# w_repr and b_repr as one replicated array, per-channel patch weights over three banks, and the bias from TensorE, in the opening of a one-layer vision tower

## The chip, the cores and the metric

The kernel runs on one core of one Trainium2 chip. The metric is the device time of one execution in microseconds, and the median of several runs counts. Before the change the median of three runs is 330.68 us, from 330.09 to 334.6 us. The engines are PE (TensorE; PEld is its weight load), DVE (VectorE), ACT (ScalarE), POOL (GpSimd) and SP (SyncE, which here only issues DMAs). A name with q (ACTq, SPq) is the sequencer of that engine.

## The reference, cut to what matters

The input is 32 images of 3 x 96 x 96, cut into 16 x 16 patches: 36 tokens an image, 1152 in all. The change touches only the first step, the tokens.

```
y = jnp.einsum('bchw,rc->bhwr', x, W_repr) + b_repr
y = y.reshape(bs, h, ph, w, pw, R)
y = y.transpose(5, 0, 1, 3, 2, 4).reshape(R, bs, h * w, ph * pw)
out = jnp.einsum('rbnp,rep->bne', y, W_proj) + b_proj.sum(axis=0)
...
h = h + attn(_layernorm(h), W_qkv, W_out)       # 12 heads of 64, over each image's 36 tokens
h = h + ffn(_layernorm(h), gate_w, gate_b, w1, b1, w2, b2)   # 8 experts of 768, one per token
```

R is 5 and the embedding is 192 wide. The first product is linear in x, so the kernel folds it: for each channel c an effective patch weight weff[c] = sum over r of W_repr[r, c] * W_proj[r], and a constant row, the bias, which is the sum over r and over the 256 pixels of b_repr[r] * W_proj[r], plus the sum of b_proj.

## The kernel before, in words

The tokens go in four blocks (NB) of 288, each in three tiles (NT) of 96. Ahead of the blocks stands an opening, which does for block 0 what block b does for block b+1: tokens, layer norm, transposition, the first query and key heads, and the values. The blocks are a hardware loop on each engine, and after them comes the expert layer over gathered tiles of 128 tokens. The order of work is written by hand, engine by engine, with semaphores between them. Each engine works through its program in order, so an instruction that waits holds up all that stands behind it on that engine.

**The opening, by engine.** SP issues the loads in order: W_repr and b_repr spread over all 128 partitions (wr, br), the patch weights (wp, 960 KB), the patches of block 0 (xb, 864 KB), b_proj, the query/key/value weights in two column pieces of two DMAs each (wq, pieces 0 and 1), W_out and the gate. wp shares its bytes with a later tile, so the trace calls it late, as it does weff. DVE makes weff for channels 0 and 1, going through r and alternating between the two channels (L936, L938). ACT makes the five scaled pieces of channel 2 (L691) and POOL adds them up (L1179). DVE then makes wb, the pixels' share of the bias (L945, L947). PE adds it over the partitions with a tile of ones (L536 to L538), and DVE copies it out of PSUM (L954). PE makes the tokens of a tile in six products (L413), which DVE takes with the bias added (L859), followed by the layer-norm statistics (L848, L850). POOL makes 1/std from them (L1196, L1199), DVE the normalised rows (L854), and PE transposes them (L421, L422). ACT rounds the transposed rows to the single-pass format (L705, L707) and DVE takes the rest (L867, L868). Only then can the heads start (L428), which are sums of five single-pass products: for them the weights too are split in a rounded part (ACT, L695, L696) and a rest (DVE, split_wq, L875 and L877).

**What runs beside it.** After its casts of wq piece 1 ACT issues the load of the first expert weights w1, two DMAs of 3072 KB (L699, L700). w1A_in shares its bytes with the scaled pieces of channel 2, so ACT also waits for weff. SP issues the patches of block 1 (L374) when all three tiles of normalised rows are there. POOL copies the tokens (keep_h, L1234) and then issues three indirect DMAs (L1211), which write single words of the expert lists to HBM. Here the ones of the opening write to spare places.

**Where w1 is needed.** In each of the first three blocks ACT rounds a third of w1 in between its attention work: round_w1 part 0 in step 1 (L715), part 1 in step 3 (L718), part 2 in step 5 (L720). Part 0 waits on one semaphore for both DMAs of w1. Behind it on ACT stand the copies of the query and key heads out of PSUM (L724, L729) and the exponentials (L737).

**Banks.** Products cycle over four PSUM banks (ACC), in the order of the list OPENING. A semaphore pair per bank says full and free. keep_clock (L523) is a row of transpositions whose results nobody reads.

## Time and profile before

| | us |
|---|---|
| median of 3 runs | 330.68 |
| lowest, highest | 330.09, 334.6 |
| profiled execution, its own time | 329.01 |
| its span | 327.3 |
| PE, DVE, ACT, POOL busy | 265.2, 202.1, 160.9, 77.0 |

Times in the trace count from the start of the span. The span is 1.7 us shorter than that execution's time, and that execution is 1.7 us shorter than the median. The mean TensorE clock over the span is 0.944 of full speed. The shares of busy time are averages over the whole kernel. The opening is only its first 28 us or so, and there each engine is busy or waits in its own pattern.

### The profile page before, as it was taken

The page shows a single profiled execution, that of the slowest core. Times are in us where ns is not written, and L with a number is a line of the kernel's source. Part 1 is how long each engine was busy: PE and PEld are TensorE (multiplying, and loading weights), DVE is VectorE, ACT ScalarE, POOL GpSimd, SP SyncE. Part 2 cuts the span into 40 slices and gives each one's busy share as a digit, 9 for nine tenths or more (in the row PEclk, how much of TensorE's full clock was granted, in tenths as well). Part 3 has the DMA queues.
Part 4 walks back from the last instruction along what each step waited for, and adds up shares of the span by engine and source line. Part 5 has one row for each costly group of instructions (what it writes and reads, how often), then busy time and mean ns, then how long its engine had stood idle before and what let it go on. Part 6 is the DMA issues. An engine that isn't in the chain of part 4 may idle for free.

```text
span 327.3 us, 6876 instructions
## 1 busy us (share of the span) xinstructions
PE 265.2 (81%) x2034; PEld 232.3 (71%) x2035; DVE 202.1 (62%) x570; ACT 160.9 (49%) x585; POOL 77.0 (24%) x123
## 2 busy tenths in 40 slices
PE   1676998899989799998799997630469999999980
PEld 1666877688978688887598876530458998989870
DVE  2986778827878918888828876334046655655620
ACT  3323488942598923598825598120024344344220
POOL 2715000103121103211003300203412334334221
PEclk9997999989999989999899999965599999999998
DMA  6899920001300003200001058880230221221100
GB/s 228 238 310 429 128 72 2 3 0 44 122 0 0 0 0 81 81 0 0 0 0 55 2 68 358 353 303 33 49 75 10 64 72 41 60 66 33 33 0 0
DMA packets 8656, 27.93 MB, mean 85 GB/s; under 512 B 4503, under 2 KB 5795, under 8 KB 7998
## 3 DMA queue, kind: packets, MB, share of 16 engines
q1 hardware_dynamic: 6078, 17.37, 17.7%
q10 hardware_dynamic: 288, 6.29, 5.3%
q0 software_dynamic: 2272, 4.04, 4.6%
q8 instruction: 9, 0.15, 0.2%
q14 instruction: 9, 0.07, 0.1%
HBM read 25.00 MB, written 3.39 MB: 87 GB/s over the span
## 4 chain that ended last, share of the span: by engine, by line
PE 57%; ACT 13%; DVE 11%; issue 9%; DMA 5%; POOL 2%; DVEq 0%; SPq 0%; ACTq 0%; POOLq 0%
PE psum L428 21%; PE psum L653 9%; PE psum L486 7%; ACT late L737 6%; PE psum L413 4%; PE psum L456 3%; PE psum L523 3%; PE psum L641 2%; DVE w1B L912 2%; DMA expert_lists<-tok_id,place_i 2%; PE psum L477 2%; DMA late<-w_proj 2%; ACT late L759 1%; PE psum L465 1%; DMA xb<-token_table,ids 1%
## 5 line engine op out<-in xcount | busy, mean ns | idle before, releaser
L737 ACT ACTIVATE late<-late,top 108x108 f32<-108x108 f32 (+1 forms) x144 | 52.5, 375 | 2.8 <-DVE top L892 2.8
L428 PE MATMUL psum<-xn_hi,wq_parts 128*128 128x288 f32 x144 | 37.0, 325 | 2.3 <-DVE xnB_lo L868 1.4
L653 PE MATMUL psum<-w2s,kT 128*128 x192 | 34.7, 330 | 2.8 <-issue 1.4
L1196 POOL TENSOR_SCALAR veps<-mv 96x1 f32<-96x1 f32 x24 | 5.6, 235 | 131.3 <-DVE mv L850 130.7
L653 PEld LDWEIGHTS psum<-w2s,kT 128*128 128x128 f32 x192 | 30.8, 190 | 4.8 <-issue 4.8
L486 PE MATMUL psum<-wo,oT 128*96 128x192 f32 x144 | 29.8, 362 | 1.1 <-ACT oT L766 1.1
L428 PEld LDWEIGHTS psum<-xn_hi,wq_parts 128*128 128x128 f32 x144 | 25.4, 196 | 4.8 <-issue 1.6
L737 ACT ACTIVATION_READ_ACCUMULATOR late<-late,top 108x1 f32 (+1 forms) x144 | 28.7, 199 | 0.0
L1257 POOL DMA_INDIRECT out<-oT,ids x16 | 16.1, 1009 | 51.6 <-DVE oT L1127 51.6
L413 PE MATMUL psum<-late,xb 128*96 128x192 f32 x144 | 25.8, 330 | 2.8 <-issue 2.8
L486 PEld LDWEIGHTS psum<-wo,oT 128*96 128x96 f32 x144 | 25.3, 183 | 2.7 <-issue 0.9
L810 ACT ACTIVATE qT<-qT 128x512 f32<-128x512 f32 (+1 forms) x32 | 15.0, 515 | 24.9 <-DVE qT L1113 24.9
L456 PE MATMUL psum<-kT,qT 64*108 64x108 f32 (+1 forms) x288 | 20.9, 263 | 5.7 <-ACT kT L729 4.0
L523 PE MATMUL psum<-ident 128*128 128x128 f32 x48 | 8.9, 372 | 20.5 <-DMA ids<-expert_lists 13.6
L413 PEld LDWEIGHTS psum<-late,xb 128*96 128x96 f32 x144 | 22.7, 163 | 3.9 <-issue 3.2
L1102 DVE TENSOR_TENSOR xnA_lo<-psum,xn_hi 128x128 fp32r<-128x128 f32 x16 | 4.7, 291 | 33.0 <-issue 22.3
L1211 POOL DMA_INDIRECT expert_lists<-tok_id,place_i x15 | 15.5, 1035 | 37.0 <-DVE place_i L1054 33.5
L886 DVE TENSOR_TENSOR late<-psum,mask 108x432 f32<-108x432 f32 (+1 forms) x36 | 19.8, 550 | 6.6 <-PE psum L456 4.6
L456 PEld LDWEIGHTS psum<-kT,qT 64*108 64x108 f32 (+1 forms) x288 | 15.1, 160 | 12.3 <-issue 8.4
L759 ACT COPY late<-psum 108x432 f32<-108x432 f32 (+1 forms) x36 | 17.3, 479 | 12.3 <-PE psum L465 12.2
L465 PE MATMUL psum<-ident,late 108*108 108x108 f32 (+1 forms) x144 | 18.2, 248 | 5.9 <-DVE late L900 5.3
L523 PEld LDWEIGHTS psum<-ident 128*128 128x128 f32 x48 | 8.5, 202 | 20.2 <-issue 20.2
(161 smaller groups left out, 642.5 us busy)
## 6 DMA issues: line engine op xcount, KB each, us to landing
w2s<-w SPq DMA_DIRECT2D x1, 4608.0 KB, 17.6
xb<-xT SPq DMA_DIRECT2D x4, 864.0 KB, 6.9
w1A_in<-w ACTq DMA_DIRECT2D x1, 3072.0 KB, 10.4
w1B_in<-w ACTq DMA_DIRECT2D x1, 3072.0 KB, 26.3
late<-b SPq DMA_DIRECT2D x2, 1536.0 KB, 9.3
token_table<-rows SPq DMA_DIRECT2D x4, 432.0 KB, 3.5
late<-w_proj SPq DMA_DIRECT2D x1, 960.0 KB, 5.4
kT<-b SPq DMA_DIRECT2D x1, 768.0 KB, 13.9
```

The source lines that it names most:

```text
L413: mm = pe.matmul(dst[0:TT, 0:D], xb[:, k, t * TT:(t + 1) * TT], weff[:, k // 2, k % 2, :], start=(k == 0), stop=(k == KX - 1))
L428: mm = pe.matmul(dst, lhsT, rhs, start=(i == 0), stop=(i == len(parts) - 1))
L456: mm = pe.matmul(psum[0:n, SC_BANKS[k], i * n:(i + 1) * n], qT[rows_, 2 * q + i, t0:t0 + n], kT[rows_, 2 * q + i, t0:t0 + n], start=True, ...
L465: mm = pe.transpose(psum[0:n, TR_BANK, i * n:(i + 1) * n], probs[0:n, u % 3, i * n:(i + 1) * n], ident[0:n, 0:n])
L486: mm = pe.matmul(dst[0:TT, 0:D], oT[:, c, t * TT:(t + 1) * TT], wo[:, c, :], start=(c == 0), stop=(c == PAIRS - 1))
L523: pe.transpose(psum[:, TR_BANK, 0:P], ident[:, :], ident[:, :])
L653: mm = pe.matmul(psum[:, 6, 0:D], hidT[i % 2][:, c * P:(c + 1) * P], w2s[:, bass.ds(e, 1), c, :], start=(c == 0), stop=(c == FCH - 1))
L737: ex = act.activation(head, head, ACT.Exp, bias=top[0:n, u % 3, i:i + 1], scale=LOGIT_SCALE, accum_out=total[0:n, u % 3, i:i + 1])
L759: act.copy(probsT[0:n, u % 3, 0:HQ * n], psum[0:n, TR_BANK, 0:HQ * n]).then_inc(tr_free, 1)
L886: dve.tensor_tensor(sc.rearrange("p (k h) n -> p k h n", k=2), psum[0:n, both, 0:2 * n].rearrange("p k (h n) -> p k h n", n=n), mask[0:n, ...
L1211: pool.indirect_dma_start(out=perm, out_offset=bass.IndirectOffsetOnAxis(ap=place_i[:, t:t + 1], axis=0), in_=tok_id[:, t:t + 1], in_offse ...
L1257: pool.indirect_dma_start(out=out, out_offset=bass.IndirectOffsetOnAxis(ap=ids[:, j:j + 1], axis=0), in_=yo[j % 4], in_offset=None, bounds ...
```

## The change

W_repr and b_repr arrive as one array of 128 equal rows of 20 numbers, laid out by the host, in one DMA in front; the DMA of b_repr, which stood between xb and b_proj, goes. The bias is no longer prepared on DVE: PE multiplies the patch weights by b_repr, read with a step of 0 over 96 columns, in ten products, and adds b_proj in an eleventh. wb goes from the program. ACT copies the bias out of PSUM, between its casts of wq pieces 0 and 1. keep_clock(32) no longer waits for the patch weights, only for the identity matrix. DVE makes weff one channel after the other, with a semaphore for each, and PE makes the tokens by channel in the order 0, 2, 1, with the sums of the three tiles in three banks. DVE's split of wq piece 0 is cut: the upper half stays ahead of the tokens, the lower one moves behind the three normalised rows.

```diff
--- before.py
+++ after.py
@@ -102,7 +102,7 @@
     return [[("tok", 1)], [("tok", 2)], [("xt", 0)], [("xt", 1)], [("xt", 2), ("o", 0)], [("o", 1), ("o", 2)]][s - 5]
 
 
-OPENING = ([("tok", 0), ("bias",), ("tok", 1), ("tok", 2)] + [("xt", t) for t in range(NT)]
+OPENING = ([("bias",), ("tok", 0), ("tok", 1), ("tok", 2)] + [("xt", t) for t in range(NT)]
            + [("q", 0), ("k", 0), ("q", 1), ("k", 1)] + [("v", g, f) for g in range(3) for f in range(2)])
 MIDDLE, FINAL = per_block_products(False), per_block_products(True)
 assert len(MIDDLE) % len(ACC) == 0
@@ -119,7 +119,7 @@
     return n % len(ACC), n // len(ACC) + blocks * (len(MIDDLE) // len(ACC))
 
 
-def build(nc, xT, w_proj, w_repr, b_repr, b_proj, w_qkv, w_out, gate_w, gate_b, w1, b1, w2, b2, out):
+def build(nc, xT, w_proj, reps, b_proj, w_qkv, w_out, gate_w, gate_b, w1, b1, w2, b2, out):
     table = nc.dram_tensor("token_table", [TOKENS + 1, 2 * D], F32, kind="Internal").ap()
     perm = nc.dram_tensor("expert_lists", [LISTS + SPARE_SLOTS, 1], U32, kind="Internal").ap()
 
@@ -144,8 +144,8 @@
         psum = ctx.enter_context(nc.psum_tensor("psum", [P, 8, 512], F32))
 
 
-        wr = sb("wr", [P, REPR * CHANNELS])
-        br = sb("br", [P, REPR])
+        wr_br = sb("wr_br", [P, REPR * CHANNELS + REPR])
+        wr, br = wr_br[:, 0:REPR * CHANNELS], wr_br[:, REPR * CHANNELS:]
         bp = sb("bp", [REPR, D])
 
         late = sb("late", [P, EXPERTS * FF])
@@ -157,7 +157,6 @@
         w_first = v_cols + 2 * p_cols
 
         weff = late[:, w_first:w_first + 2 * CHANNELS * D].rearrange("p (c h e) -> p c h e", c=CHANNELS, h=2)
-        wb = sb("wb", [P, 2, D])
         bias = sb("bias", [TT, D])
 
         w2s, wq_in, wq_parts = sb_shared(("w2s", [P, EXPERTS, FCH, D], F32), ("wq_in", [P, 4, 3 * HD], F32),
@@ -294,9 +293,8 @@
         waited = {"dve": sem("dve_waited"), "pool": sem("pool_waited")}
         ident_ready = sem("ident_ready")
         consts_ready = sem("consts_ready")
-        weff_ready = sem("weff_ready")
+        weff_ready = [sem(f"weff_ready{c}") for c in range(CHANNELS)]
         scaled = sem("scaled")
-        wb_ready = sem("wb_ready")
 
         tiles_ready = sem("tiles_ready")
         ids_here = [sem(f"ids_here{j}") for j in range(FFT)]
@@ -350,10 +348,9 @@
         @block.sync
         def _(sp):
             sp.sem_inc(rows_sent, 16)
-            sp.dma_start(wr[:, :], w_repr.partition_broadcast(P)).then_inc(wp_here, 16)
+            sp.dma_start(wr_br[:, :], reps).then_inc(wp_here, 16)
             sp.dma_start(wp, w_proj).then_inc(wp_here, 16)
             sp.dma_start(xb[:, :, :], xT[0]).then_inc(x_here, 16)
-            sp.dma_start(br[:, :], b_repr.partition_broadcast(P)).then_inc(br_here, 16)
             sp.dma_start(bp[:, :], b_proj).then_inc(br_here, 16)
             for i, cols in enumerate(WQ_PIECES):
                 sp.dma_start(wqA_in[:, cols], w_qkv[0:DA, cols]).then_inc(wq_here[i], 16)
@@ -524,20 +521,30 @@
 
 
             pe.wait_ge(ident_ready, 1)
+            keep_clock(32)
+
             pe.wait_ge(wp_here, 32)
-            keep_clock(32)
-            pe.wait_ge(x_here, 16)
-            pe.wait_ge(weff_ready, 2)
-            tokens(0, product(("tok", 0), 0, opening=True))
-            pe.wait_ge(br_here, 32)
-            pe.wait_ge(wb_ready, 1)
             slot = product(("bias",), 0, opening=True)
             dst = into(slot)
-            pe.matmul(dst[0:TT, 0:D], ones[:, :], wb[:, 0, :], start=True, stop=False)
-            pe.matmul(dst[0:TT, 0:D], ones[:, :], wb[:, 1, :], start=False, stop=False)
+            for r in range(REPR):
+                for i in range(2):
+                    pe.matmul(dst[0:TT, 0:D], br[:, r:r + 1].to_broadcast([P, TT]), wp[:, i, r, :],
+                              start=(r == 0 and i == 0), stop=False)
+            pe.wait_ge(br_here, 16)
             pe.matmul(dst[0:TT, 0:D], ones[0:REPR, :], bp[:, :], start=False, stop=True).then_inc(full[slot[0]], 1)
-            for t in range(1, NT):
-                tokens(t, product(("tok", t), 0, opening=True))
+
+            pe.wait_ge(x_here, 16)
+            order = [0, 2, 1]
+            for c in order:
+                pe.wait_ge(weff_ready[c], 1)
+                for t in range(NT):
+                    slot = product(("tok", t), 0, opening=True)
+                    dst = into(slot) if c == order[0] else acc(slot[0])
+                    for i in range(2):
+                        mm = pe.matmul(dst[0:TT, 0:D], xb[:, 2 * c + i, t * TT:(t + 1) * TT], weff[:, c, i, :],
+                                       start=(c == order[0] and i == 0), stop=(c == order[-1] and i == 1))
+                    if c == order[-1]:
+                        mm.then_inc(full[slot[0]], 1)
             for t in range(NT):
                 turn_xn(t, product(("xt", t), 0, opening=True), (xn_ready, t + 1), xn, 0)
             pe.wait_ge(wq_hi_ready, 2)
@@ -694,8 +701,12 @@
                 act.wait_ge(wq_here[i], 32)
                 act.copy(wqA_hi[:, cols], wqA_in[:, cols]).then_inc(wq_hi_ready, 1)
                 act.copy(wqB[0:DB, cols], wqB_in[0:DB, cols]).then_inc(wq_hi_ready, 1)
-
-            act.wait_ge(weff_ready, 2)
+                if i == 0:
+                    slot = product(("bias",), 0, opening=True)
+                    complete(act, slot)
+                    act.copy(bias[:, :], acc(slot[0])[0:TT, 0:D]).then_inc(free[slot[0]], 1)
+
+            act.wait_ge(weff_ready[CHANNELS - 1], 1)
             act.dma_start(w1A_in[:, :], w1[0:DA, :]).then_inc(w1_here, 16)
             act.dma_start(w1B_in[:, :], w1[DA:DA + 2 * DB, :]).then_inc(w1_here, 16)
 
@@ -868,11 +879,15 @@
                 dve.tensor_tensor(xnB_lo[:, ts], src[0:DB, TT:2 * TT], xnB[0:DB, ts],
                                   ALU.subtract).then_inc(free[slot[0]], 1)
 
-            def split_wq(i):
+            def split_wqA(i):
 
                 cols = WQ_PIECES[i]
                 dve.wait_ge(wq_hi_ready, 2 * i + 1)
                 dve.tensor_tensor(wqA_lo[:, cols], wqA_in[:, cols], wqA_hi[:, cols], ALU.subtract).then_inc(wq_split, 1)
+
+            def split_wqB(i):
+
+                cols = WQ_PIECES[i]
                 dve.wait_ge(wq_hi_ready, 2 * i + 2)
                 dve.tensor_tensor(wqB[DB:2 * DB, cols], wqB_in[0:DB, cols], wqB[0:DB, cols],
                                   ALU.subtract).then_inc(wq_split, 1)
@@ -929,37 +944,29 @@
             dve.memset(xnB_lo2[DB:2 * DB, :].bitcast(F32), 0.0)
 
             dve.wait_ge(wp_here, 32)
-            for r in range(REPR):
-                for c in range(CHANNELS - 1):
+            for c in range(CHANNELS - 1):
+                for r in range(REPR):
                     s = r * CHANNELS + c
                     if r == 0:
-                        ins = dve.tensor_scalar(weff[:, c, :, :], wp[:, :, r, :], wr[:, s:s + 1], None, ALU.mult)
+                        own(dve.tensor_scalar(weff[:, c, :, :], wp[:, :, r, :], wr[:, s:s + 1], None, ALU.mult))
                     else:
                         ins = dve.scalar_tensor_tensor(weff[:, c, :, :], wp[:, :, r, :], wr[:, s:s + 1],
                                                        weff[:, c, :, :], ALU.mult, ALU.add)
-                own(ins)
-            dve.engine_nop().then_inc(weff_ready, 1)
-            dve.wait_ge(br_here, 32)
-            for r in range(REPR):
-                if r == 0:
-                    ins = dve.tensor_scalar(wb[:, :, :], wp[:, :, r, :], br[:, r:r + 1], None, ALU.mult)
-                else:
-                    ins = dve.scalar_tensor_tensor(wb[:, :, :], wp[:, :, r, :], br[:, r:r + 1], wb[:, :, :],
-                                                   ALU.mult, ALU.add)
-                own(ins)
-            dve.engine_nop().then_inc(wb_ready, 1)
-            split_wq(0)
-            slot = product(("bias",), 0, opening=True)
-            complete(dve, slot)
-            dve.tensor_copy(bias[:, :], acc(slot[0])[0:TT, 0:D]).then_inc(free[slot[0]], 1)
-            taken(dve, slot)
+                        if r < REPR - 1:
+                            own(ins)
+                        else:
+                            ins.then_inc(weff_ready[c], 1)
+            split_wqA(0)
+            taken(dve, product(("bias",), 0, opening=True))
             for t in range(NT):
                 take_tokens(t, product(("tok", t), 0, opening=True))
             for t in range(NT):
                 layernorm(xn[:, t, :], h[:, t, :], 0, t, t).then_inc(xn_ready, 1)
+            split_wqB(0)
             for t in range(NT):
                 take_xn_lo(t, product(("xt", t), 0, opening=True), t)
-            split_wq(1)
+            split_wqA(1)
+            split_wqB(1)
 
             dve.wait_ge(consts_ready, 1)
             own(dve.tensor_copy(iota[:, :], iota_i[:, :]))
@@ -1176,9 +1183,12 @@
 
             for r in range(1, REPR):
                 pool.wait_ge(scaled, r + 1)
-                own(pool.tensor_tensor(weff[:, CHANNELS - 1, :, :], wp_last[:, 0, :, :] if r == 1 else
-                                       weff[:, CHANNELS - 1, :, :], wp_last[:, r, :, :], ALU.add))
-            pool.engine_nop().then_inc(weff_ready, 1)
+                ins = pool.tensor_tensor(weff[:, CHANNELS - 1, :, :], wp_last[:, 0, :, :] if r == 1 else
+                                         weff[:, CHANNELS - 1, :, :], wp_last[:, r, :, :], ALU.add)
+                if r < REPR - 1:
+                    own(ins)
+                else:
+                    ins.then_inc(weff_ready[CHANNELS - 1], 1)
             pool.affine_select(out=before[:, :], in_=before[:, :], compare_op=ALU.is_gt, fill=0.0, base=0,
                                pattern=[[1, TT]], channel_multiplier=-1)
             images = GMAX // PER_IMAGE
@@ -1279,8 +1289,7 @@
         "xT": np.asarray(x).reshape(NB, per, CHANNELS, GRID, 2, half, GRID, PATCH)
         .transpose(0, 5, 7, 2, 4, 1, 3, 6).reshape(NB, P, KX, BT),
         "w_proj": np.asarray(L0_tok_W_proj).reshape(REPR, D, 2, P).transpose(3, 2, 0, 1),
-        "w_repr": np.asarray(L0_tok_W_repr).reshape(REPR * CHANNELS),
-        "b_repr": np.asarray(L0_tok_b_repr),
+        "reps": np.tile(np.r_[np.asarray(L0_tok_W_repr).reshape(-1), np.asarray(L0_tok_b_repr)], (P, 1)),
         "b_proj": np.asarray(L0_tok_b_proj),
         "w_qkv": np.asarray(L0_attn_W_qkv).T,
         "w_out": np.asarray(L0_attn_W_out).T.reshape(PAIRS, P, D).transpose(1, 0, 2),
```

On TensorE the opening stood so before:

```order
L523 MATMUL psum<-ident 128x128 x32
L413 MATMUL psum<-late,xb 96x192 x6
L536 MATMUL psum<-wb,ones 96x192
L537 MATMUL psum<-wb,ones 96x192
L538 MATMUL psum<-bp,ones 96x192
L413 MATMUL psum<-late,xb 96x192 x12
L421 MATMUL psum<-ident,rows 128x96
```

and so with the change (L531 multiplies the patch weights by b_repr, L544 are the tokens):

```order
L520 MATMUL psum<-ident 128x128 x32
L531 MATMUL psum<-late,wr_br 96x192 x10
L534 MATMUL psum<-bp,ones 96x192
L544 MATMUL psum<-late,xb 96x192 x18
L418 MATMUL psum<-ident,rows 128x96
```

The bias now stands ahead of all token products, and the 18 token products follow each other with a wait at every channel.

On VectorE the stretch from the patch weights to the rest of the first transposed tile stood so before (wq_parts are the two splits of piece 0):

```order
L936 TENSOR_SCALAR late<-late,wr 128x384 x2
L938 SCALAR_TENSOR_TENSOR late<-late,wr 128x384 x8
L941 ISA
L945 TENSOR_SCALAR wb<-late,br 128x384
L947 SCALAR_TENSOR_TENSOR wb<-late,br,wb 128x384 x4
L950 ISA
L875 TENSOR_TENSOR wq_parts<-wq_in,wq_parts 128x1024
L877 TENSOR_TENSOR wq_parts<-wq_in,wq_parts 64x1024
L954 COPY bias<-psum 96x192
L859 TENSOR_TENSOR h<-psum,bias 96x192
L848 BN_STATS stats<-h 96x6
L850 BN_AGGR mv<-stats 96x2
```

and so with the change (L886 is the upper split, L892 the lower one; the rows of the second and third tile of tokens are left out between the pieces):

```order
L951 TENSOR_SCALAR late<-late,wr_br 128x384
L953 SCALAR_TENSOR_TENSOR late<-late,wr_br 128x384 x4
L951 TENSOR_SCALAR late<-late,wr_br 128x384
L953 SCALAR_TENSOR_TENSOR late<-late,wr_br 128x384 x4
L886 TENSOR_TENSOR wq_parts<-wq_in,wq_parts 128x1024
L870 TENSOR_TENSOR h<-psum,bias 96x192
...
L865 TENSOR_SCALAR rows<-h,mv,rstd 96x192 x3
L892 TENSOR_TENSOR wq_parts<-wq_in,wq_parts 64x1024
L878 TENSOR_TENSOR xnA_lo<-psum,xn_hi 128x96
```

The five instructions of wb and the copy of the bias are gone from VectorE, and the lower split stands directly ahead of the work on the transposed tiles.

## Rows read from the trace of the kernel before

**Rows 1.** Chain that ended last, 40 to 75 us: start, us, what.

```profile
43.26 1.46 ACT late L737 x8
44.72 0.01 ACTq L715
44.77 0.08 ACT w1A_hi L715
...
53.35 0.42 ACT kT L729
```

**Rows 2.** Instructions on w1B_in, and time from issue to landing.

```profile
L700 ACTq DMA_DIRECT2D w1B_in<-w x1: 446/446/446, 18.3 to 18.3; - x1
...
DMA to landing us min/median/max: 26.3/26.3/26.3
```

**Rows 3.** Windows: engines' busy time, then PEclk, DMA share, GB/s.

```profile
6.00:8.00 2.00, 1.07 (x5) 1.10 (x6) 1.15 (x3) 1.18 (x3) 0.00 (x0) 1.00 0.98 405
...
8.50:9.00 0.50, 0.50 (x4) 0.50 (x3) 0.50 (x1) 0.50 (x2) 0.50 (x1) 1.00 0.03 1
...
19.00:33.00 14.00, 10.51 (x58) 9.35 (x57) 9.96 (x26) 4.70 (x15) 6.48 (x10) 0.88 1.02 408
...
34.00:36.00 2.00, 2.00 (x16) 1.61 (x16) 1.93 (x5) 0.61 (x3) 0.00 (x0) 1.00 1.87 93
...
38.00:40.00 2.00, 2.00 (x15) 1.83 (x14) 1.42 (x5) 0.93 (x6) 0.00 (x0) 1.00 0.32 35
```

**Rows 4.** Timeline of DVE, opening: start, us, line, op, [idle before <- releaser].

```profile
7.60 7.45 DVE L938 SCALAR_TENSOR_TENSOR late<-late,wr 128x384 f32<-128x384 f32 x8
15.10 0.42 DVE L945 TENSOR_SCALAR wb<-late,br 128x384 f32<-128x384 f32 x1
15.55 2.58 DVE L947 SCALAR_TENSOR_TENSOR wb<-late,br,wb 128x384 f32<-128x384 f32 x4
...
19.43 1.22 DVE L877 TENSOR_TENSOR wq_parts<-wq_in,wq_parts 64x1024 fp32r<-64x1024 f32 x1
...
21.07 0.35 DVE L859 TENSOR_TENSOR h<-psum,bias 96x192 f32<-96x192 f32 x1
...
22.05 0.32 DVE L859 TENSOR_TENSOR h<-psum,bias 96x192 f32<-96x192 f32 x1
...
24.64 0.18 DVE L850 BATCH_NORM_AGGREGATE mv<-stats 96x2 f32<-96x6 f32 x1
...
25.92 0.38 DVE L854 TENSOR_SCALAR rows<-h,mv,rstd 96x192 f32<-96x192 f32 x1 [0.54 <-POOL rstd L1199]
...
27.71 0.24 DVE L868 TENSOR_TENSOR xnB_lo<-psum,xn_hi 64x96 fp32r<-64x96 f32 x1
```

**Rows 5.** Timeline of POOL, opening.

```profile
9.17 3.73 POOL L1179 TENSOR_TENSOR late<-late,w1A_in 128x384 f32<-128x384 f32 x3
...
27.59 1.19 POOL L1211 DMA_INDIRECT expert_lists<-tok_id,place_i  x1 [0.46 <-issue]
```

**Rows 6.** Timeline of ACT and its sequencer, opening.

```profile
14.04 1.05 ACT L695 CAST wq_parts<-wq_in 128x1024 fp32r<-128x1024 f32 x1 [4.58 <-DMA wq_in<-w_qkv]
...
17.89 0.39 ACTq L699 DMA_DIRECT2D w1A_in<-w  x1
```

**Rows 7.** Timeline of PE, opening.

```profile
6.93 5.50 PE L523 MATMUL psum<-ident 128*128 128x128 f32 x32 [6.93 <-DMA late<-w_proj]
...
19.57 4.14 PE L413 MATMUL psum<-late,xb 128*96 128x192 f32 x24
...
28.20 0.58 PE L428 MATMUL psum<-xn_hi,wq_parts 128*128 128x288 f32 x1 [1.41 <-DVE xnB_lo L868]
```

**Rows 8.** Issues of xb by SP in the blocks, and time to landing.

```profile
L374 SPq DMA_DIRECT2D xb<-xT x3: 357/363/364, 26.5 to 128.2; - x3
...
DMA to landing us min/median/max: 6.6/6.7/21.1
```

**Rows 9.** Windows around the first heads: busy times, then PEclk, DMA share, GB/s.

```profile
28.20:31.20 3.00, 3.00 (x13) 3.00 (x13) 2.90 (x5) 0.62 (x2) 2.39 (x3) 0.51 0.95 410
31.20:44.70 13.50, 13.31 (x104) 11.57 (x103) 9.27 (x23) 7.58 (x32) 0.46 (x1) 1.00 0.90 174
```

## The prediction

> **What bounds the kernel now.** I read the chain of waits first, then the timelines of the opening by engine, then what the chain rests on in the next 20 us. The opening is serial: PE's first head product starts at 28.20 us and had waited for DVE's last piece of the transposed rows [rows 7], which starts at 27.71 us [rows 4]. DVE is the engine to follow up to there. It makes the patch weights until 15.05 us, then wb, both lower and upper split, the bias copy, and takes the first tokens at 21.07 us. From there one tile costs 0.98 us (22.05 - 21.07), the third waits for PE, and the third normalised tile waits for POOL until 25.92 us [rows 4]. So whatever leaves DVE between 15.05 and 21.07 us brings the first heads forward.
>
> The second thing to see decides what that is worth. In step 1 of block 0 ACT reaches the rounding of w1. The chain goes through it: exponentials until 44.72 us, a sequencer instruction, the cast at 44.77 us, and then ACT's own work up to the key copy at 53.35 us [rows 1]. The second w1 DMA was issued at 18.3 us and took 26.3 us [rows 2], so it landed at 44.6 us. ACT came 0.1 us after its data. **There is no slack in that load**: an ACT that comes earlier waits. And the load is slow. Until 33 us the DMA engines move 408 GB/s; then the rate drops to 93 GB/s and 35 GB/s with the engines mostly not busy [rows 3]. w1 and the next patches are 6.29 + 0.88 = 7.17 MB; 14 us at 408 GB/s are 5.7 MB, so 1.46 MB were left at 33 us, 3.6 us of work at that rate, and they took 11. The drought cost 7 to 8 us. It sets in after POOL's three word-wise indirect DMAs, the first issued at 27.59 us [rows 5]; the patches of block 1, issued at 26.5 us, needed 21.1 us where the others need 6.6 [rows 8]. That the two belong together is a guess from the order in time.
>
> **The change part by part.**
>
> *DVE, patch weights.* Eight scalar-tensor-tensor operations take 7.45 us, 0.93 us each [rows 4], while POOL adds channel 2 until 12.90 us [rows 5]; the four of wb, without POOL, take 2.58 us, 0.65 each. Going channel by channel makes each depend on the one before. The wb ones already did, and show gaps of about 0.03 us; before, half of these pairs had no such wait, so at most 4 x 0.03 = 0.1 us more. Channel 0 is ready at about 7.2 + 4 x 0.93 = 10.9 us, channel 2 at 12.9, channel 1 at 15.1.
>
> *DVE, what goes.* wb with its gaps: 18.17 - 15.10 = 3.07 us; the lower split 1.22, and what lies between its end and the first tokens, the bias copy, 21.07 - 20.65 = 0.42 [rows 4]. Together 4.7 us ahead of the tokens. So the first tokens are taken at 15.1 + 1.25 = 16.35 us. ACT's upper cast, on which that split waits, ended at 15.09 us [rows 6], and its wq piece should come earlier (below). ACT then copies the bias after its lower cast, at about 15.2 to 16.4 us. That is new work of 0.35 us on ACT, hidden, because ACT then waits for wq piece 1.
>
> *PE.* The bias is eleven products. Twenty-four token products took 4.14 us, 0.17 each [rows 7], so 1.9 us, or 3.8 at half the clock. I take the weight load with a step of 0 at the price of an ordinary one; the trace has none, and the bounds are 0 and, at thrice the price, 5.7 us. They start when the patch weights are there, at 6.8 us, and even the upper bound, 12.5 us, leaves the tokens by channel time: channel 1 comes last, at 15.1 us. Then only 6 of 18 products are left, 1.0 us, or 2.1 at half clock. The first tile is full at 15.5 to 15.8 us, the last at 16.1 to 17.2; DVE wants them at 16.35, 17.3 and 18.3. **So PE goes off the path**, and DVE's wait for the third tile goes too.
>
> *POOL and the normalised rows.* The third tile's statistics end at 19.3 us instead of 24.82. From there to the third normalised row's start it was 25.92 - 24.82 = 1.1 us [rows 4], so 20.4 to 20.5 us, 5.4 us earlier than before.
>
> *The lower split.* It now runs from 20.85 to 22.1 us. Its cover is the transposition and ACT's rounding, which run beside it: the last rest of the third tile starts 1.4 us after its row ended (27.71 - 26.30) [rows 4]. But the rests of tiles 0 and 1, which used to fit in between, now wait. Three pairs in a row take about 1.2 us, to 23.3 us, against 27.95. The first head product comes at 23.5 us instead of 28.2: **4.7 us gained at that point**.
>
> *The clock.* The heads started at the lower of the two levels, 0.51 over their first 3.0 us, and ran at full clock after [rows 9]. PE had then been idle for 1.4 us, and mostly since its token products ended at 23.7 [rows 7]. With the change it does only six short transpositions between about 17 and 23.5 us, so the heads again start at 1.2 GHz, and may need as long as the first products of all did. Those start at 6.93 us; 32 of them take 5.50 us. I charge 0.3 us. Gain at the heads: 4.4 us.
> The Trainium skill, "TensorE: Matmul & The Clock Gate", section on the clock gate, says that an idle PE falls back to the lower level and gets the higher one only after sustained work. By that rule warming up at 1.8 us instead of 6.9 us, and then waiting for channels, wins nothing for the heads: all 20 query and key products of the opening would run at 1.2 GHz, where here about 12 did. The trace agrees that the heads start low; it has no row for how long they would stay so after a longer idle time.
>
> *The DMA queue.* The small DMA of b_repr is gone, 128 rows of 20 bytes between xb and the rest. While it is served the rate falls from 405 GB/s to 1 GB/s [rows 3]. The first array grows from 60 to 80 bytes a row, with as many rows: nothing. b_proj stays small. So the wq pieces come up to 1.0 us earlier (bounds 0 and 1.5, the length of the dip), and with piece 1 so does the issue of w1, which was tied to it at 17.89 us [rows 6]: 16.9 us.
>
> *The landing of w1.* The patches of block 1 are issued 5.4 us earlier, POOL's indirect DMAs as well, so both fall in the middle of w1. The bytes are the same, and if the drought is the same it only comes earlier. Then w1 lands when the sum of all is through, 1.0 us before 44.6: at 43.6 us. ACT would be there at 44.7 - 4.4 = 40.3 us. It waits 3.3 us, and behind it wait the head copies and exponentials, and with them PE. **Net gain 44.7 - 43.6 = 1.1 us** of the 4.4. Without the removed DMA it would be 0.1.
>
> Against the profiled execution that is 329.0 - 1.1 = 327.9 us. The median lies 1.7 us above that execution, so 329.6 us. Of that offset I take 1.4, since the median of only three runs is drawn up by one high one: 329.3 us.
>
> **The rivals.**
>
> *The load is not late (the full gain).* If the drought does not come, or is shorter, when the indirect DMAs meet w1 in full flow, then w1 is through at 33 + 3.6 - 1.0 = 35.6 us and ACT never waits. Then 4.4 us count: 330.7 - 4.4 = 326.3 us. For it: the rate is low while the DMA engines are idle, so it is a latency or a pile-up, not bytes, and may depend on the moment. Against it: the indirect DMAs come in any case, and w1 has then more to go.
>
> *The load is later (slower).* The collision now happens with some 3 MB of w1 still to come instead of 1.5. The point from which it decides is 44.7 us: each us of landing beyond it is a us lost. The patches of block 1 landed at 26.5 + 21.1 = 47.6 us [rows 8]; if w1 shared that fate, the kernel would lose 2.9 us and give 333.6 us. For it: the droughts' length is not known, and 334.6 us was seen among the three runs. Against it: in the trace the two loads end their burst together, and nothing says that more bytes make a drought longer.
>
> *The opening does not get shorter by 4.4 us.* The one way is PE: if the step-0 weight loads or a low clock throughout put the bias and tokens behind DVE, the last tile would come after 18.3 us. That needs 1.1 us more than the lowest clock gives. It would cost 1 or 2 of the 4.4 us, which the wait for w1 mostly hides: 329.3 to 330.7 us.
>
> **How the numbers follow.** The forecast (w1 lands about 1 us earlier, 328.5 to 330.5 us) has a chance of 0.45, the full gain (325.0 to 328 us) 0.33, the later load 0.14, the opening that is not shorter 0.08. The range from 325.0 to 332.5 us takes in the first two and the last with their bounds, and the milder half of the third. 2% of the median are 6.6 us, about what a measurement can tell from no change. Faster by more needs more than the opening gives in any case: 0.03. Slower by more needs w1 landing beyond 51 us: 0.03. Within: 0.94.
>
> **What would show it.** In the new trace the first token is taken at about 16.4 us, the first head product starts at 23.2 to 24 us, w1 is issued near 16.9 us. Then the step on which all rests: ACT idle for about 3 us ahead of its cast of w1 in block 0, released by the DMA. If that idle time is missing and the cast starts near 40.3 us, the rival of the full gain holds; if the cast starts after 44.8 us, the slower one. A first head product after 25 us would say that I mis-costed DVE or PE.

## The result: 1.5% slower, and the profile after

| us | before | after |
|---|---|---|
| median of 4 runs | 330.38 | 335.86 |
| lowest, highest | 329.48, 334.6 | 334.05, 336.3 |
| profiled execution | 329.01 | 335.99 |
| its span, mean granted clock | 327.3, 0.944 | 334.0, 0.906 |

The ratio is 1.0154, with an interval of [1.0098, 1.021]. It was forecast to be a little faster, 329.3 us, in a range from 325.0 to 332.5. All ratios here leave out runs that are more than 1.5% above the fastest of the same kernel, while the medians keep them.

The opening did what it was to do. The timeline of DVE and of PE after, against [rows 4] and [rows 7] (start, length, line, operation, [idle before it <- releaser]):

```profile
16.22 0.35 DVE L870 TENSOR_TENSOR h<-psum,bias 96x192 f32<-96x192 f32 x1
...
20.30 0.37 DVE L865 TENSOR_SCALAR rows<-h,mv,rstd 96x192 f32<-96x192 f32 x1 [0.54 <-POOL rstd L1209]
20.71 1.22 DVE L892 TENSOR_TENSOR wq_parts<-wq_in,wq_parts 64x1024 fp32r<-64x1024 f32 x1
...
22.79 0.23 DVE L879 TENSOR_TENSOR xnB_lo<-psum,xn_hi 64x96 fp32r<-64x96 f32 x1
```

```profile
6.89 3.41 PE L531 MATMUL psum<-late,wr_br 128*96 128x192 f32 x20
...
15.21 2.19 PE L544 MATMUL psum<-late,xb 128*96 128x192 f32 x12 [0.25 <-DVE late L953]
...
23.27 0.58 PE L425 MATMUL psum<-xn_hi,wq_parts 128*128 128x288 f32 x1 [2.10 <-DVE xnB_lo L879]
```

The first tokens come 4.85 us earlier and the first head product 4.93 us earlier (28.20 to 23.27). Then the lead is lost. The timeline of ACT and its sequencer after (w1A_in and w1B_in are the two halves of w1; the cast waits for both):

```profile
16.66 0.45 ACTq L711 DMA_DIRECT2D w1B_in<-w  x1
...
46.88 1.90 ACT L726 CAST w1A_hi<-w1A_in  x1 [5.89 <-DMA w1B_in<-w]
...
96.28 1.88 ACT L726 CAST w1A_hi<-w1A_in  x1
```

ACT reaches the cast of w1 at 40.99 us (46.88 - 5.89), 3.7 us earlier than before, and stands idle for 5.89 us. w1 was issued 1.66 us earlier and landed 2.2 us later: 30.1 us after its issue instead of 26.3 [rows 2]. The chain of waits now goes through the load itself, where it went through ACT's exponentials [rows 1]:

```profile
16.22 0.40 ACT wq_parts L702
16.62 0.04 issue
16.66 30.10 DMA w1B_in<-w
46.76 0.02 issue
46.78 0.06 ACTq L726
```

The windows show what PE did meanwhile (busy time of PE, PEld, DVE, ACT, POOL, then the granted clock, the DMA share and GB/s):

```profile
26.00:28.00 2.00, 2.00 (x11) 2.00 (x10) 0.38 (x3) 0.80 (x2) 1.65 (x2) 0.50 0.97 410
...
32.00:36.00 4.00, 4.00 (x26) 3.65 (x25) 3.39 (x8) 2.84 (x16) 0.00 (x0) 1.00 0.91 86
36.00:40.00 4.00, 3.81 (x37) 3.27 (x36) 2.65 (x9) 2.46 (x8) 0.00 (x0) 1.00 0.41 75
40.00:42.00 2.00, 2.00 (x25) 1.72 (x25) 1.84 (x5) 0.99 (x6) 0.00 (x0) 1.00 1.01 405
42.00:44.00 2.00, 1.74 (x16) 1.40 (x12) 0.00 (x0) 0.00 (x0) 0.00 (x0) 1.00 0.12 41
44.00:46.00 2.00, 0.00 (x0) 0.00 (x0) 0.00 (x0) 0.00 (x0) 0.00 (x0) 0.99 0.00 0
46.00:48.00 2.00, 0.00 (x0) 0.00 (x0) 0.00 (x0) 1.12 (x1) 0.00 (x0) 0.50 0.00 0
...
49.60:56.20 6.60, 6.56 (x35) 5.68 (x36) 5.34 (x12) 6.27 (x23) 0.00 (x0) 0.50 0.00 0
```

Three things are to be seen. The fall of the rate (the drought) is there as before [rows 3], but starts at about 31 us and lasts about 9. When the rate is back, the last packets of w1 start at 42.5 us, and w1 is reported complete only at 46.76. And PE, idle from 43.7 to 49.6 us, falls to 1.2 GHz at 46.0 and works at it until 56.2 us, full of work. Before, the same stretch was at full clock:

```profile
46.00:56.20 10.20, 8.77 (x78) 7.76 (x79) 8.34 (x20) 9.71 (x36) 0.80 (x2) 1.00 0.01 2
```

The DMA share in such a table must be read with care: a window counts a packet whole, with its bytes and its time, if the packet starts in it. That is why [rows 3] can show a share of 1.87. Taken over the whole drought, after and then before, the share is near 1:

```profile
30.00:43.00 13.00, 12.81 (x108) 11.08 (x105) 9.82 (x24) 6.62 (x29) 0.00 (x0) 1.00 0.95 154
```

```profile
33.00:44.00 11.00, 10.81 (x86) 9.18 (x85) 8.46 (x20) 5.90 (x26) 0.00 (x0) 1.00 0.90 133
```

So the DMA engines are not idle in the drought. They are occupied by packets that take long: of w1's packets of 24 KB, most of which take 0.9 us, single ones last up to 8.0 us after and 7.5 us before (the trace's records of single packets).

**Where the 6.7 us of span went.** The cast of w1 in block 1 and the first indirect DMA of the last expert lists, before, and the latter after:

```profile
92.39 1.89 ACT L715 CAST w1A_hi<-w1A_in  x1
...
221.14 1.02 POOL L1211 DMA_INDIRECT expert_lists<-tok_id,place_i  x1 [7.75 <-DVE place_i L1054]
```

```profile
228.43 1.02 POOL L1221 DMA_INDIRECT expert_lists<-tok_id,place_i  x1 [8.59 <-DVE place_i L1061]
```

Block 1's cast of w1 starts at 96.28 us, 3.9 us later than before. Of these 2.1 stood already at the cast in block 0, 46.88 against 44.77 [rows 1]; the low clock behind the idle time is the best candidate for the other 1.8. (Between e1 and e6 below, which differ by the wait alone, the lag grows likewise, from 6.65 us at the cast in block 0 to 8.9 in block 1; between e11 and e10 it hardly grows, from 9.8 to 10.1. So the size of this part is not settled.) A further 3.4 us come later: the first indirect DMA of the last expert lists starts 7.3 us later than before. There a second low stretch lies, which the profiled execution before lacked:

```profile
196.00:203.00 7.00, 5.44 (x72) 4.16 (x68) 5.79 (x16) 7.00 (x35) 0.00 (x0) 1.00 0.77 169
203.00:210.00 7.00, 6.53 (x34) 5.17 (x35) 2.33 (x7) 4.01 (x18) 0.00 (x0) 0.51 0.97 418
```

The expert layer gives some 0.6 us back. The 3.4 us go with that stretch, which comes without the change too. All profiles have a long low stretch around the last lists; some have an extra one ahead of it, as after has. From block 1's cast to the last lists the seven with the extra stretch (after, e1, e2, e4, e5, e6, e8) take 132.2 to 134.9 us, the ten without it (before, e3, e7, e9 to e15) 128.8 to 130.2. Kernels with and without the change stand in both groups.

### The profile page after: what moved, and what is told of

It reads as the page before. It is cut to its first block, busy times and chain, and to the rows that moved or that the text cites. A ratio compares the mean times of both kernels' runs of the same rounds, so it can differ in the third digit from the quotient of the medians.

```text
span 334.0 us, 6898 instructions
## 1 busy us (share of the span) xinstructions
PE 275.7 (83%) x2050; PEld 241.1 (72%) x2051; DVE 198.7 (60%) x564; ACT 161.7 (48%) x586; POOL 79.0 (24%) x123
## 3 DMA queue, kind: packets, MB, share of 16 engines
q1 hardware_dynamic: 5934, 17.37, 16.7%
## 4 chain that ended last, share of the span: by engine, by line
PE 55%; DMA 16%; DVE 11%; ACT 7%; issue 6%; POOL 2%; SPq 1%; DVEq 0%; POOLq 0%; ACTq 0%
PE psum L425 19%; PE psum L660 10%; DMA w1B_in<-w 9%; PE psum L483 7%; DMA wq_in<-w_qkv 3%; PE psum L453 3%; ACT late L748 3%; PE psum L410 3%; PE psum L474 3%; PE psum L648 3%; DVE w1B L927 2%; PE psum L462 2%; DMA expert_lists<-tok_id,place_i 2%; DVE top L906 1%; DVE late L901 1%
## 5 line engine op out<-in xcount | busy, mean ns | idle before, releaser
L425 PE MATMUL psum<-xn_hi,wq_parts 128*128 128x288 f32 x144 | 38.2, 334 | 2.9 <-DVE xnB_lo L879 2.1
L483 PE MATMUL psum<-wo,oT 128*96 128x192 f32 x144 | 31.3, 375 | 0.8 <-ACT oT L777 0.8
L425 PEld LDWEIGHTS psum<-xn_hi,wq_parts 128*128 128x128 f32 x144 | 26.3, 203 | 5.6 <-issue 2.3
L462 PE MATMUL psum<-ident,late 108*108 108x108 f32 (+1 forms) x144 | 20.0, 267 | 11.7 <-ACT late L770 5.9
L483 PEld LDWEIGHTS psum<-wo,oT 128*96 128x96 f32 x144 | 26.0, 189 | 2.9 <-issue 0.9
L462 PEld LDWEIGHTS psum<-ident,late 108*108 108x108 f32 (+1 forms) x144 | 15.6, 138 | 14.7 <-issue 7.1
L1221 POOL DMA_INDIRECT expert_lists<-tok_id,place_i x15 | 16.8, 1117 | 37.5 <-DVE place_i L1061 34.3
L770 ACT COPY late<-psum 108x432 f32<-108x432 f32 (+1 forms) x36 | 17.2, 476 | 15.8 <-PE psum L462 15.7
L453 PE MATMUL psum<-kT,qT 64*108 64x108 f32 (+1 forms) x288 | 21.2, 267 | 4.0 <-ACT kT L740 3.6
L901 DVE TENSOR_TENSOR late<-psum,mask 108x432 f32<-108x432 f32 (+1 forms) x36 | 19.8, 550 | 5.5 <-PE psum L453 5.4
L453 PEld LDWEIGHTS psum<-kT,qT 64*108 64x108 f32 (+1 forms) x288 | 15.4, 163 | 10.5 <-issue 7.6
L425 PE MATMUL psum<-wq_parts,xn_hi 128*108 128x384 f32 (+1 forms) x72 | 21.6, 354 | 0.0
L474 PE MATMUL psum<-late 108*64 108x108 f32 (+1 forms) x288 | 21.2, 272 | 0.0
## 6 DMA issues: line engine op xcount, KB each, us to landing
w2s<-w SPq DMA_DIRECT2D x1, 4608.0 KB, 17.2
w1B_in<-w ACTq DMA_DIRECT2D x1, 3072.0 KB, 30.1
```

The costliest lines, as they stand in the source:

```text
L425: mm = pe.matmul(dst, lhsT, rhs, start=(i == 0), stop=(i == len(parts) - 1))
L453: mm = pe.matmul(psum[0:n, SC_BANKS[k], i * n:(i + 1) * n], qT[rows_, 2 * q + i, t0:t0 + n], kT[rows_, 2 * q + i, t0:t0 + n], start=True, ...
L462: mm = pe.transpose(psum[0:n, TR_BANK, i * n:(i + 1) * n], probs[0:n, u % 3, i * n:(i + 1) * n], ident[0:n, 0:n])
L474: mm = pe.matmul(psum[rows_, AV_BANK, i * n:(i + 1) * n], v[0:n, g, col:col + DH], probsT[0:n, u % 3, at:at + n], start=True, stop=True)
L483: mm = pe.matmul(dst[0:TT, 0:D], oT[:, c, t * TT:(t + 1) * TT], wo[:, c, :], start=(c == 0), stop=(c == PAIRS - 1))
L770: act.copy(probsT[0:n, u % 3, 0:HQ * n], psum[0:n, TR_BANK, 0:HQ * n]).then_inc(tr_free, 1)
```

## The experiments

The runs form four groups, each on one chip: e1 to e4, e5 to e8, e9 to e12, e13 to e15. The kernel before had medians of 334.4, 332.6, 334.8 and 332.4 us there, so ratios are to be compared, not times. The ratio of one kernel, too, moves by a percent or so from group to group, and each trace is of one execution. All edits are against the changed kernel, if nothing else is said. Columns: the issue of the second w1 DMA, its landing after issue, ACT's w1 cast in block 0 and the idle time before it that ended with the load.

| run | median us | ratio to before [95%] | issue | takes | cast | idle |
|---|---|---|---|---|---|---|
| after | 335.86 | 1.0154 [1.0098, 1.021] | 16.7 | 30.1 | 46.88 | 5.89 |
| e1 no dummies | 330.35 | 0.9986 [0.9933, 1.0039] | 15.3 | 20.8 | 40.82 | 0 |
| e2 before, no dummies | 334.57 | 1.0025 [0.9956, 1.0094] | 18.2 | 19.1 | 46.00 | 0 |
| e3 dummies after w1 | 329.38 | 0.9892 [0.9833, 0.9951] | 15.3 | 21.2 | 39.61 | 0 |
| e4 patches later | 340.86 | 1.0243 [1.0096, 1.039] | 18.1 | 32 | 50.08 | 9.06 |
| e6 e1, w1 at 29 us | 338.05 | 1.0161 [1.0094, 1.0227] | 29.2 | 18.2 | 47.47 | 6.48 |
| e7 before, one array | 334.5 | 1.0038 [0.9996, 1.0079] | 15.3 | 23.5 | 44.81 | 0 |
| e8 e3 and filler | 324.5 | 0.9734 [0.9671, 0.9797] | 16.7 | 19.5 | 38.80 | 0 |
| e9 before, as e8 | 331.15 | 0.9934 [0.9885, 0.9984] | 18.9 | 19.4 | 43.44 | 0 |
| e10 filler alone | 337.09 | 1.0105 [1.0059, 1.0151] | 16.1 | 32 | 48.05 | 9.61 |
| e11 e1 and filler | 326.18 | 0.9756 [0.9667, 0.9845] | 15.8 | 19.7 | 38.23 | 0 |
| e12 e8 again | 326.86 | 0.9796 [0.9686, 0.9905] | 15.4 | 19.8 | 38.27 | 0 |
| e13 e1, words by POOL | 337.24 | 1.0145 [1.0003, 1.0288] | 17.2 | 31.0 | 48.33 | 7.16 |
| e14 e1, rows by POOL | 326.55 | 0.9824 [0.9691, 0.9957] | 15.9 | 21.0 | 39.59 | 0 |
| e15 e1, words by SP | 326.28 | 0.9815 [0.9673, 0.9958] | 15.5 | 25.3 | 40.93 | 0.19 |

The changed kernel again (e5) had a median of 341.73 us, from 336.07 to 342.23, and no ratio is given for it. Its profile, of the run of 341.37 us, has w1 landing 32.2 us after its issue and the cast at 48.97 us behind 8.64 idle. The late landing of after is thus there again, and somewhat longer.

> The changed kernel itself, unedited, as a control beside the others on one chip. Theory A: w1 lands at 44 to 50 us, ACT waits 3 us or more for it, the time is 3 to 7 us above the kernels without indirect DMAs in w1's flow. Theory C (the loss of the first comparison was the day's): w1 lands before 43 us and the time is that of the kernel before.

**What makes w1 late: the word-wise indirect DMAs (e1 to e4).** POOL's three indirect DMAs of the opening write to spare places, so a kernel can do without them. In e1 they go, and in e2 the kernel before loses them too. (Both then also send each block's own lists later in the block; e3 does not.)

```diff
-            pool.iota(place_i[:, :], pattern=[[TT, NT]], base=LISTS, channel_multiplier=1)
-            pool.memset(tok_id[:, :], SPARE_ROW).then_inc(place_ready, 1)
+            pool.sem_inc(lists_free, 1)
...
             def body(b, last):
-                send_places(b)
...
                     keep_h(b + 1)
+                    send_places(b)
+                    pool.wait_ge(lists_sent, 16 * NT * (b + 1))
+                    pool.sem_inc(lists_free, 1)
```

> The changed kernel without POOL's three word-wise indirect DMAs of the opening (which write only to spare places); POOL itself waits for each block's own three and tells DVE. Theory A (these three DMAs cause the drought, and their slow writes hold back the completions of w1): no drought, w1 lands at 34 to 37 us, ACT reaches its w1 cast at about 41 us and does not wait, PE's clock stays high in block 0, time 324 to 327 us. Theory B (the drought comes from the patches of block 1 running into w1, whoever else is there): w1 lands at 44 us or later again, ACT waits 3 us or more, time 333 us or more. Theory C (w1 is late, but the 5 us are lost elsewhere): no wait at w1, yet 331 us or more.

> The kernel before without the same three indirect DMAs. Theory A: w1 lands at 35 to 38 us instead of 44.6, but ACT gets to it only at 44.7 us, so the time hardly moves: 328.5 to 330.5 us. The difference between this and the changed kernel without them is then the 4 to 4.7 us that the opening gained. Theory B: w1 still lands near 44.6 us, time 329 to 331 us as well, but then the changed kernel without them is not faster than this one.

In e3 they stay, but wait for w1: `pool.wait_ge(w1_here, 32)` behind keep_h(0). In e4 SP issues the patches of block 1 later, at 26.7 us instead of 20.9: `complete(sp, product(("k", 0), 0, opening=True))` ahead of its loop.

> The changed kernel, where POOL issues the three indirect DMAs of the opening only once w1 has landed (all else the same). Theory A: w1 lands at 34 to 37 us, no wait on ACT, 324 to 328 us. Theory B: w1 as late as in the changed kernel (46 us), 334 to 336 us; then the order of the indirect DMAs against w1 does not matter.

> The changed kernel, where SP issues the patches of block 1 only after the first key head is in PSUM, some 5 us later than in the changed kernel, about when the kernel before issued them. Theory A: little changes, w1 lands at 44 to 47 us and the time is 333 to 336 us. Theory B: most of the loss goes, w1 lands before 43 us, time below 330 us.

Without them in its way w1 takes 19.1 to 21.2 us, in either kernel, and nobody waits. With the patches 5.8 us later it takes 32. The windows of e3 show no drought, the rate holds until the bytes are through:

```profile
30.00:32.00 2.00, 2.00 (x17) 1.88 (x18) 1.90 (x5) 1.58 (x8) 0.00 (x0) 1.00 0.95 409
32.00:34.00 2.00, 2.00 (x14) 1.65 (x13) 1.65 (x4) 1.59 (x8) 0.00 (x0) 1.00 0.96 410
34.00:36.00 2.00, 2.00 (x16) 1.91 (x15) 1.34 (x3) 0.80 (x2) 0.00 (x0) 1.00 0.07 29
```

So the guess in the prediction that drought and indirect DMAs belong together is shown, and the patches are cleared. In e1 and e3 they are issued as early as after, at 20.7 us, and w1 is not held up. Their own 25.1 us of landing after, 14.4 in e1, are suffered, not caused. Letting them leave later (e4) helps nothing. Its 50.08 us at the cast against after's 46.88 is not shown to be their doing either, since after itself had 48.97 in e5.

The price is also shown. Within one group e1 and e3 are at 0.9986 and 0.9892, and e4, which has the words in the load, at 1.0243. e1 is 1.7% below after in ratio, and all of the change's loss is gone. But e1 is no faster than before. In the profiles its lead over before is 4.9 us at block 1's cast (87.47, 92.39) and nothing at the last lists (221.35, 221.14): a low stretch of the clock lies between, at 196 to 203 us. e3 has the same lead in block 1 (87.34), lacks that stretch, and keeps 4.2 us (216.91). e2, where before also loses its dummies, gains nothing, as it must if w1 had landed 0.1 us before ACT came. Its cast is even later than before's, 46.00: its heads ran at 0.50 until 34 us, against 31.2 before. The landings are those of theory A. The times are not: e1 to e4 lie 1.4 to 4.9 us above what theory A gave, in part since the kernel before itself stood higher in this group (334.4).

**A late w1 alone, without any words (e6).** e1, with the two issues of w1 moved behind ACT's work on the first heads.

```diff
-            act.dma_start(w1A_in[:, :], w1[0:DA, :]).then_inc(w1_here, 16)
-            act.dma_start(w1B_in[:, :], w1[DA:DA + 2 * DB, :]).then_inc(w1_here, 16)
...
+            act.dma_start(w1A_in[:, :], w1[0:DA, :]).then_inc(w1_here, 16)
+            act.dma_start(w1B_in[:, :], w1[DA:DA + 2 * DB, :]).then_inc(w1_here, 16)
```

> The changed kernel without the three indirect DMAs of the opening, but with w1 issued only after the opening's last key copy (28 to 29 us instead of 16.7), so that it lands late with no drought at all. Theory A (what costs is the wait of ACT for w1 and the clock that PE loses meanwhile, nothing else of the drought): w1 lands at 44 to 47 us, ACT idles 4 to 6 us, PE's clock falls in block 0, and the time is that of the changed kernel, 333 to 337 us. Theory D (the drought also costs elsewhere, in other transfers): the same landing, yet 331 us or less.

The load arrives at 47.4 us at full rate, and the kernel is as slow as after: 1.0161 against 1.0154. ACT's cast, and PE behind it:

```profile
47.47 1.90 ACT L725 CAST w1A_hi<-w1A_in  x1 [6.48 <-DMA w1B_in<-w]
```

```profile
34.00:40.00 6.00, 5.81 (x50) 5.02 (x49) 4.13 (x11) 3.54 (x14) 0.00 (x0) 1.00 1.03 440
...
50.00:56.00 6.00, 5.77 (x34) 5.03 (x35) 5.54 (x12) 6.00 (x23) 0.00 (x0) 0.55 0.00 0
```

6.65 us of lateness (47.47 - 40.82 of e1) cost 1.75% of the run (1.0161 - 0.9986), 5.8 us. So a late landing by itself, with no words in it, is enough to cost all that the change lost, and the low clock comes with the wait.

**The array alone (e7).** The kernel before, with W_repr and b_repr in one DMA.

```diff
-            sp.dma_start(wr[:, :], w_repr.partition_broadcast(P)).then_inc(wp_here, 16)
+            sp.dma_start(wr_br[:, :], reps).then_inc(wp_here, 16)
...
-            sp.dma_start(br[:, :], b_repr.partition_broadcast(P)).then_inc(br_here, 16)
...
-            pe.wait_ge(br_here, 32)
+            pe.wait_ge(br_here, 16)
```

> The kernel before with one part of the change alone: w_repr and b_repr as one replicated array in one DMA; the bias stays on DVE and PE, the order stays. Theory A: w1 is issued 1.0 to 1.7 us earlier (16.2 to 16.9 us), the first heads start at 28 us as before, nothing else moves, ratio to the kernel before 0.99 to 1.005. Rival (the loss sits in the new array): ratio above 1.01.

w1 is issued at 15.3 us, 3.0 us earlier than in the profile of before, and lands at 38.8. How much of the 3.0 us is the array's doing is uncertain: thirteen profiles with the array have the issue at 15.3 to 18.1 us, the three without it (before, e2, e9) at 18.2 to 18.9. It buys nothing (1.0038), since ACT comes at 44.8 as before. The landing says more:

```profile
DMA to landing us min/median/max: 23.5/23.5/23.5
```

POOL's first indirect DMA is at 27.59 us here, 12.3 us after w1's issue. Before it is 9.3 us after it, and w1 takes 26.3; after it is 6.0 (22.64 - 16.66), and w1 takes 30.1. Among the profiles with the words 4.8 to 6.5 us behind the issue (after, e4, e5, e10, e13) w1 takes 30.1 to 32.2 us, in no order. So, from one profile each at 12.3 and 9.3 us and five at about 6, the words cost more when they come nearer to the start of the load. The earlier opening moved them to the worse place.

**The clock (e8 to e12).** After, the clock is at 1.2 GHz from 22.1 to 28.9 us, and the heads start in it, at 23.27. Before, this low stretch was 3.4 us long, from 27.7 to 31.2. e8 is e3 with unread transpositions around the six of the normalised rows; e9 gives the same to before, with 12 and 10; e10 gives 16 and 16 to after, e11 to e1; e12 repeats e8 on another chip.

```diff
+            keep_clock(16)
             for t in range(NT):
                 turn_xn(t, product(("xt", t), 0, opening=True), (xn_ready, t + 1), xn, 0)
+            keep_clock(16)
```

> The changed kernel with the indirect DMAs of the opening after w1, and 16 unread transpositions on PE ahead of the transposition of the rows and 16 more ahead of the first heads. Theory A: w1 lands by 37 us; the heads run at full clock, so the 20 products take 2.7 us instead of 4.9, and the time is 1 to 3 us below the kernel without these transpositions: 326 to 328.5 us, if the later dips of the clock stay where they were. Rival: the dips move elsewhere and the gain is below 1 us.

> The kernel before, with the two edits that made the changed kernel fast: the indirect DMAs of the opening after w1, and unread transpositions (12 and 10) around the transposition of the rows. Theory A: the first heads start at 28.2 us and run at full clock, w1 is no limit; 1 to 2 us below the kernel before. The changed kernel with the same two edits is then 4 to 6 us below this one, which is what the change itself is worth once w1 is out of its way. Rival (the two edits alone do it): the two differ by less than 2 us.

> The changed kernel with the unread transpositions only (16 and 16), the indirect DMAs where the change has them. Theory A: the heads run at full clock and ACT reaches w1 2 us earlier, but w1 still lands at 46 us or later, so ACT waits 2 us longer and the time is that of the changed kernel, ratio to the kernel before above 1.01. Theory E (the low clock of the heads was the loss): 2 us or more below the changed kernel, ratio 1.005 or less.

> The changed kernel without the three indirect DMAs of the opening and with the unread transpositions (16 and 16). Theory A: the same as with the indirect DMAs after w1, 323 to 328 us; POOL has less to do, but is on no path there.

> The best version so far (the changed kernel, indirect DMAs after w1, 16 and 16 unread transpositions) once more, on the chip of the three others, for comparison with them. Theory A: 323 to 328 us, ratio to the kernel before 0.965 to 0.985.

In e12 the first head product takes 0.38 us instead of 0.58, and the window of the heads is at the higher level:

```profile
23.08 0.38 PE L425 MATMUL psum<-xn_hi,wq_parts 128*128 128x288 f32 x1 [0.35 <-DVE xnB_lo L881]
```

```profile
23.00:28.00 5.00, 4.92 (x36) 4.49 (x37) 4.07 (x7) 1.60 (x4) 0.00 (x0) 1.00 1.01 433
```

With w1 out of the way the filler brings ACT to its cast at 38.2 to 38.8 us (e8, e11, e12), where it was 39.6 and 40.8 (e3, e1). In ratio e3 becomes e8, 0.9892 to 0.9734, and e1 becomes e11, 0.9986 to 0.9756. But these pairs ran on different chips, and e14 and e15 below, which have no filler, reach 0.9824 and 0.9815 with two runs each. How much of the 1.6 and 2.3% is the filler's is not shown. With w1 in the way the filler is worthless: in e10 ACT only waits longer, 9.61 us.

e9 against e12, both on one chip and both with late words and filler, is the worth of the change itself. The ratios differ by 1.4% (0.9934, 0.9796), 4.6 us. The profiles differ by 5.2 us at the cast (43.44, 38.27) and 5.0 us at the last lists (221.06, 216.06), near to the 4.4 that the prediction reckoned for the heads. (Nine of e9's ten runs took 328.5 to 333.3 us, the tenth 453.4, which is not explained.)

e10 also shows the end of the load most plainly. From 41.5 us no packet starts, and w1 lands at 48.03:

```profile
41.00:42.00 1.00, 0.20 (x2) 0.00 (x0) 0.00 (x0) 0.00 (x0) 0.00 (x0) 1.00 0.35 57
42.00:48.00 6.00, 0.00 (x0) 0.00 (x0) 0.00 (x0) 0.00 (x0) 0.00 (x0) 0.81 0.00 0
```

```profile
48.05 1.90 ACT L728 CAST w1A_hi<-w1A_in  x1 [9.61 <-DMA w1B_in<-w]
```

**Words, or POOL's way of writing them (e13 to e15)?** The base is e1, in which POOL writes three times to a scratch tensor where the dummies stood: 96 single words each in e13, 96 rows of 512 bytes in e14. In e15 SP writes three times 96 words to the spare places by plain DMAs.

```diff
+            for t in range(NT):
+                pool.indirect_dma_start(out=scratch,
+                                        out_offset=bass.IndirectOffsetOnAxis(ap=at[:, t:t + 1], axis=0),
+                                        in_=ident[0:TT, 0:1], in_offset=None).then_inc(words_sent, 16)
```

In e14 the slice is `ident[0:TT, 0:128]`. e15 has this on SP, ahead of the patches:

```diff
+            for c in range(3):
+                sp.dma_start(perm[LISTS + c * P:LISTS + c * P + TT, :], spare[0:TT, c:c + 1]).then_inc(words_sent, 16)
```

> The changed kernel without the three indirect DMAs to the expert lists, and in their place three indirect DMAs of 96 single words each from POOL to a scratch array in HBM. If words or the POOL path do it: w1 lands at 44 to 49 us as in the changed kernel, 334 to 341 us. If the expert lists as a target do it: w1 by 38 us, 328 to 332 us.

> As before, but each of the 3 x 96 indirect writes is a row of 512 bytes. If the small size of the writes does it: w1 by 38 us, no drought, 328 to 332 us. If the POOL path does it: w1 at 44 us or later, 334 us or more.

> The changed kernel without POOL's three indirect DMAs of the opening; in their place SP issues three plain DMAs of 96 single words each to the same spare places, at about 21 us. If single words do it: w1 at 42 us or later, 333 us or more. If the POOL path does it: w1 by 38 us, 328 to 332 us.

The target does not matter: e13 writes elsewhere and behaves as after does (31.0 us, 1.0145). The shape of the writes does: with the same number of them, by the same engine at nearly the same times (22.59 us in e14, 22.84 in e13), the rows leave w1 at 21.0 us. (The words are also neighbours in memory, 4 bytes apart, while the rows are 512 bytes apart. Words far from each other were not tried, so the nearness may count and not the width.) Time from issue to landing of the indirect writes themselves, in e13 and then in e14:

```profile
DMA to landing us min/median/max: 12.9/16.8/20.8
```

```profile
DMA to landing us min/median/max: 9.0/9.7/9.8
```

And the windows, of e13 in the drought, then of e14, which has none:

```profile
34.00:36.00 2.00, 2.00 (x15) 1.73 (x14) 1.45 (x4) 1.25 (x8) 0.00 (x0) 1.00 1.34 91
36.00:38.00 2.00, 2.00 (x22) 1.76 (x20) 0.99 (x3) 1.16 (x3) 0.00 (x0) 1.00 0.55 35
```

```profile
30.00:32.00 2.00, 2.00 (x17) 1.88 (x16) 1.90 (x6) 1.58 (x8) 0.00 (x0) 1.00 1.10 457
32.00:34.00 2.00, 2.00 (x14) 1.65 (x13) 1.61 (x4) 1.59 (x8) 0.00 (x0) 1.00 1.02 433
```

e15 lies between: 25.3 us and dips of the rate, 4 to 6 us more than without words, 5 less than with POOL's. Neither of the two expectations for it held: w1 landed at 40.9 us, and the time was 326.28 us.

```profile
28.00:30.00 2.00, 2.00 (x15) 1.58 (x15) 0.58 (x2) 0.40 (x1) 0.00 (x0) 0.85 0.58 86
...
38.00:40.00 2.00, 1.81 (x19) 1.49 (x18) 1.73 (x6) 1.51 (x7) 0.00 (x0) 1.00 0.82 28
```

So single words slowed this bulk load whoever wrote them, and POOL's indirect ones most (31.0 us against 25.3 and 21.0). The Trainium skill, "DMA: Bandwidth & Descriptors", Specifications, asks for transfers of 512 bytes at least and says that an engine does a read-modify-write below that; e13 against e14 agrees as to the size, and no run here shows the read-modify-write itself. That page's section "Queues, rings and completion order" says that the semaphore increment of a DMA lands only after every earlier write of the same DMA engine, across its queues. The 5.9 us in e10 from the end of w1's last packet to the completion agree with a tail of slow writes in front of it: without words in the load this gap is 0.4 to 0.7 us (e1, e2, e3, e6, e9), with rows 0.6 (e14), and with words 1.1 to 5.9. No run shows which write it is.

## Why the prediction was wrong

- **The DVE, PE and POOL steps of the opening** held: tokens 16.22 us (16.35 forecast), third row 20.30 (20.4 to 20.5), lower split at 20.71 (20.85), first head product 23.27 (23.5). The prediction's sums for PE were half of what they should be. In the trace each of these products stands as two records (24 for the 12 products of two tiles), and it took a record for a product. The bias's ten products took 3.41 us where 1.7 were reckoned, the last six token products 2.19 instead of 1.0. The last tile was full at 17.4 us, beyond the forecast's 16.1 to 17.2, and DVE took it only at 18.17, so PE was off the path all the same. The step of 0 cost nothing: 0.17 us a record, as for the tokens.
- **The clock of the heads** was charged 0.3 us, and 1.2 us were lost there: 4.93 us gained at the first product, 3.73 at ACT's arrival (44.72 to 40.99). The low stretch around the first heads was 6.8 us long instead of 3.4. That the heads would again start low was foreseen, its price not. With filler in both kernels nothing is lost there (5.2 us at the cast, e9 and e12).
- **The DMA queue:** w1's issue came 1.66 us earlier where 1.0 was taken, a little over the upper bound of 1.5, but within the scatter of that issue (e7).
- **The failed step is "The bytes are the same, and if the drought is the same it only comes earlier": w1 lands at 43.6 us.** It landed at 46.76. The drought is not a fixed 11 us to be moved about. It is made by the words (e1, e3, e13), and costs more when they come nearer to the start of the load (w1 takes 23.5 us, 26.3, and 30.1 to 32.2). The change moved the words by 4.95 us and w1 by 1.66, and so brought them 3.3 us nearer to it. Part of the loss is not in the bytes at all. w1's last packet ended at 42.8 us before and at 43.5 after, and the completion came 1.9 and 3.3 us behind it. The prediction had seen the words ahead of the drought, called the link a guess, and gave it no term. The term -1.1 us became +2.1 at the cast, 3.2 of the 8.1 us by which the profiled time missed its forecast of 327.9.
- **The DMA engines "mostly not busy", "the rate is low while the DMA engines are idle"** was a misreading of [rows 3]. They were occupied at 0.90 over the drought, by packets of up to 7.5 us. The 7 to 8 us that the drought was said to cost are right: e2 lands w1 at 37.3 us instead of 44.6.
- **The price of a wait was counted as its own length only.** "Each us of landing beyond it is a us lost" left out that PE falls to 1.2 GHz while it waits. By block 1 2.1 us had become 3.9. These 1.8 us, the 3.4 of the later low stretch, 0.3 outside the span, less the 0.6 that the expert layer gave back, are the rest of the miss. That the 3.4 fell into this profile was chance as far as is known. The slower time does not rest on them: e10 and e13 have a late w1 and no such stretch, and are at 1.0105 and 1.0145.
- **The slower rival** had the mechanism, its sign and its mark: the cast started after 44.8 us. It got 0.14, because "nothing says that more bytes make a drought longer"; true, but nothing said the contrary either. Its price of 2.9 us was too small by half: the median rose by 5.5.
- **The rival of the full gain** is refuted as a forecast, and shown as what was to be had: with w1 at 35 to 37 us ACT never waits (e1, e3, e8, e11, e12, e14).

What stays open: how words hold up the packets of a load, and POOL's more than SP's; whether words far apart would do the same; and what sets the second low stretch. It is in after (203 to 210 us) and in six others, starting between 194 and 206, with and without the change. No run controlled where it falls. The kernel before alone took 329.2 to 341.4 us in the four groups, so such things come without the change.

The versions that beat both kernels are the changed one without words in the load of w1 and with the filler: 0.9734, 0.9756 and 0.9796 of before (e8, e11, e12). The intervals of e14 and e15, which have no filler, overlap with theirs.

## What to carry to other kernels

Before work is brought forward, look at what it triggers: a DMA that is issued earlier may fall into a bulk load, and a load with no slack turns each gain ahead of it into a wait. Keep DMAs of single words out of the time of a bulk load, or make their rows 512 bytes. A wait of several us on PE's path costs its own length and then the low clock behind it. And before a table of windows is said to show idle DMA engines, ask for the whole stretch in one window. A packet of 8 us is counted in the one in which it starts.

## What the runs showed of the hardware

- 288 words of 4 bytes by POOL's indirect DMAs stretch a load of 6.3 MB from 18 to 21 us to 23.5 (e7), 26.3 (before) and 30 to 32; 288 rows of 512 bytes do not (21.0), and 288 words by SP's plain DMAs take it to 25.3.
- In that time the 16 DMA engines stay occupied (0.95 of 30 to 43 us in after), while single packets of 24 KB last up to 8.0 us instead of 0.9.
- A load beside such words can be complete 3.3 us (after, 43.5 and 46.76) to 5.9 us (e10, 42.2 and 48.03) after the end of its last packet; without words it is 0.4 to 0.7.
- While a DMA of 128 rows of 20 bytes stood between two loads, the rate fell to 1 GB/s for half a microsecond [rows 3]; after, without it, it is 410 GB/s there (8.5 to 9 us).
- PE idle for 5.9 us was granted 1.2 GHz for the next 6.6 us of dense work, to 56.2 us, and 2.4 GHz after.
